# A Mamba-2 mixer inside a four-phase kernel: shorter, reordered lists for three engines in its head, and one silu tile finished during the scan

## The reference, cut to what matters

```
zxbcdt = layernorm(x) @ in_proj_w.T            # z: 512, xBC: 640, dt: 4 columns
dt  = softplus(zxbcdt[..., -4:] + dt_bias)     # one value for each token and head
xBC = silu(causal_conv1d(xBC, conv_w, 4 taps) + conv_b)
xs, B, C = split(xBC)                          # xs: 4 heads x 128
y, _ = ssd_scan(xs * dt, A * dt, B, C)         # A = -exp(A_log)
y = y + xs * D
g = y * silu(z)
g = g * rsqrt(mean(g * g) + 1e-5) * norm_w
x = x + g @ out_proj_w.T
```

## Time and profile before

| | us |
|---|---|
| median of 3 runs (lowest, highest) | 521.13 (520.99, 521.2) |
| the profiled execution | 521.09 |
| its span, first to last instruction | 519.3 |
| mean granted TensorE clock | 0.999 |

### The profile page before, as it was taken

The page is one execution under the profiler, slowest core; times in us unless marked ns, Lnnn a source line. Parts: engine busy times, 40 slices in busy tenths (PEclk is TensorE's granted clock), DMA queues, the critical chain, the costliest instruction groups (busy, mean ns, idle before and its releaser), DMA issues.

```text
span 519.3 us, 9035 instructions
## 1 busy us (share of the span) xinstructions
PE 503.5 (97%) x2950; PEld 426.7 (82%) x2951; DVE 406.6 (78%) x895; ACT 313.2 (60%) x784; POOL 145.6 (28%) x285
## 2 busy tenths in 40 slices
PE   6999999999999999999999999989999999999996
PEld 5778899999999988678888888867989768888885
DVE  5736567667666789899999899985888879899777
ACT  4656878688687754574534445899873365344342
POOL 1432434345243320020110111379554020020110
PEclk9999999999999999999999999999999999999999
DMA  7320100000000303100030000000000000000101
GB/s 278 125 81 3 40 2 2 1 1 2 2 2 8 151 2 107 42 1 1 0 141 2 2 0 1 1 2 1 1 2 1 0 1 1 1 0 1 40 2 40
DMA packets 5933, 14.17 MB, mean 27 GB/s; under 512 B 640, under 2 KB 3200, under 8 KB 5888
## 3 DMA queue, kind: packets, MB, share of 16 engines
q1 hardware_dynamic: 5888, 13.60, 7.5%
HBM read 12.55 MB, written 1.05 MB: 26 GB/s over the span
## 4 chain that ended last, share of the span: by engine, by line
PE 79%; DVE 12%; issue 3%; ACT 3%; DMA 1%; POOL 1%; SPq 0%; DVEq 0%; ACTq 0%; POOLq 0%
PE psum L172 61%; PE psum L493 4%; DVE xs L1994 2%; PE psum L525 2%; PE psum L1809 1%; PE psum L241 1%; DMA w_raw<-in_wk 1%; PE psum L1813 1%; PE psum L1819 1%; DVE f_t L1315 1%; DVE ln_stats L214 1%; DVE xn L234 1%; PE psum L1836 1%; PE psum L486 1%; ACT f_sil L1201 1%
## 5 line engine op out<-in xcount | busy, mean ns | idle before, releaser
L172 PE MATMUL psum<-xT_hl,ffn_w_hl 128*128 128x512 f32 x312 | 77.7, 395 | 0.7 <-ACT f_sil L1201 0.6
L172 PE MATMUL psum<-f_um,ffn_w_hl 128*128 128x512 f32 x288 | 72.8, 399 | 1.1 <-DVE f_t L1315 0.6
L172 PEld LDWEIGHTS psum<-xT_hl,ffn_w_hl 128*128 128x128 f32 x312 | 56.2, 188 | 13.1 <-DVE ffn_w_hl L916 1.1
L172 PEld LDWEIGHTS psum<-f_um,ffn_w_hl 128*128 128x128 f32 x288 | 53.1, 188 | 15.0 <-DVE f_um L1327 1.7
L1201 ACT ACTIVATE f_sil<-psum 128x512 f32<-128x512 f32 (+1 forms) x48 | 28.4, 596 | 49.5 <-PE psum L172 49.4
L1225 ACT ACTIVATE f_ch_hl<-f_ch 128x512 fp32r<-128x512 f32 x48 | 30.3, 631 | 41.7 <-DVE f_ch L1384 40.0
L172 PE MATMUL psum<-xT_hl,wq_hl 128*128 128x512 f32 x192 | 52.0, 407 | 0.6 <-ACT qT L593 0.6
L172 PE MATMUL psum<-wo_hl,oT_hl 128*128 128x256 f32 x384 | 50.5, 281 | 1.0 <-DVE oT_hl L726 0.6
L172 PEld LDWEIGHTS psum<-wo_hl,oT_hl 128*128 128x128 f32 x384 | 47.7, 188 | 3.5 <-DVE oT_hl L726 1.1
L593 ACT ACTIVATE qT<-psum 128x512 f32<-128x512 f32 x32 | 35.3, 1104 | 22.6 <-PE psum L172 22.4
L602 ACT ACTIVATE probs<-probs,small 120x66 f32<-120x66 f32 x120 | 39.9, 338 | 8.2 <-DVE small L703 8.2
(11 more groups left out here) (265 smaller groups left out, 1147.6 us busy)
## 6 DMA issues: line engine op xcount, KB each, us to landing
w_raw<-in_wq SPq DMA_DIRECT2D x4, 512.0 KB, 3.9
w_raw<-in_wo SPq DMA_DIRECT2D x4, 512.0 KB, 3.3
ffn_w_raw<-in_ffn SPq DMA_DIRECT2D x3, 576.0 KB, 5.8
ffn_w_raw_far<-in_ffn SPq DMA_DIRECT2D x3, 576.0 KB, 5.4
ssd_w_raw<-in_ssd SPq DMA_DIRECT2D x3, 512.0 KB, 5.3
x_resid<-in_x SPq DMA_DIRECT2D x2, 512.0 KB, 5.2
out_x<-x_resid SPq DMA_DIRECT2D x4, 256.0 KB, 2.1
w_raw<-in_wk SPq DMA_DIRECT2D x1, 512.0 KB, 6.3
```

What stands on the lines that cost most here:

```text
L172: i = e.matmul(dst, lhs(a), rhs(b), start=start and n == 0, stop=stop and n == len(TERMS) - 1, **kw)
```

## The change

Four things are edited, all in `mixer`:

- **Convolution.** DVE no longer does tap (0, 3). ACT writes bank 0 times that tap into a new tile `far` right after `last_tap(0)` (`far_taps`), and POOL adds it (`far_adds`). `silu(0)` waits for POOL's add, and bank 0 is free for `in_proj(9)` after tap (0, 2).
- **Softplus.** ACT's ln and the steps that guard it go. POOL computes it as a series in t = e / (e + 2): 15 dependent steps in place of 11, with `ident_r` and `mask_r` made ahead of them. The reciprocal follows two taps of tile 4 and waits for POOL's second step. PE puts `in_proj(16)` ahead of the cumulative sums, DVE takes them over three taps later, and ACT's order of taps and silus changes.
- **Last convolution tile.** ACT's head ends with `silu(8)`. Tile 9 gets a tanh in the scan's second chunk (`late_tanh`, i = 1), POOL turns it into a sigmoid (`late_sigmoid`, ahead of `gate(1)`) and multiplies (`late_silu`, behind it). PE's transposes of chunk 4 and ACT's second `xs_D` half, now at i = 4, wait for it.
- **POOL's order.** `join(1)` to `join(4)` move ahead of `make_xd(1)`, with `join(2)` ahead of `rhs_col`; `make_xd(3)` moves from the head into chunk 0, and 6, 7 and 8 from chunks 0, 1 and 2 (ahead of `gate`) to behind `gate` in chunk 1 (tile 6) and chunk 3 (tiles 7 and 8).

```
+            FAR = 1
+            far = at("far_taps", [P, FAR, HALF], F32, A_W)
-            DT_DONE = 11
+            DT_DONE = 15
...
-                for n in range(12, 16):
+                for n in range(12, 17):
                     in_proj(e, n)
                 e.wait_ge(S["dt_pool"], DT_DONE)
...
-                for n in range(16, 2 * NB):
+                for n in range(17, 2 * NB):
...
+                    if c == HT:
+                        e.wait_ge(S["sl"], NC)
                     for h in range(NH):
                         m = e.transpose(bank(3)[:, tile(h)], xs[:, h, tile(c)], ident)
...
+                        conv_done(e, NC - 2)
+                        keep_busy(4, 6)
+                        e.wait_ge(S["sl"], NC - 1)
+                        keep_busy(7, 6)
                         conv_done(e, NC - 1)
-                        keep_busy(4, 6)
-                        e.wait_ge(S["sl"], NC)
-                        keep_busy(7, 6)
                         e.wait_ge(S["L"], 1)
                         keep_busy(6, 6)
...
+                def far_taps():
+                    for n in range(FAR):
+                        tap = PR_CW + n
+                        e.activation(far[:, n, :], bank(IN_BANK[0]), ACT.Copy, scale=par[:, tap:tap + 1]).then_inc(S["tap"], 1)
...
                 last_tap(12)
-                e.wait_ge(S["dt_pool"], 2)
-                e.activation(L1, U1, ACT.Ln).then_inc(S["dt_act"], 1)
+                silu(2)
                 last_tap(13)
+                silu(3)
                 last_tap(14)
-                silu(2)
+                last_tap(15)
                 silu_z(16)
-                silu(3)
-                last_tap(15)
-                silu_z(17)
                 silu(4)
                 silu(5)
+                silu_z(17)
+                silu(6)
                 silu_z(18)
-                silu(6)
+                silu(7)
                 silu_z(19)
-                for i in range(7, NC):
+                for i in range(8, NC - 1):
                     silu(i)
+
+                def late_tanh():
+                    b, h = order[convs[NC - 1]]
+                    e.wait_ge(S["join"], CONVS.index(b) + 1)
+                    e.activation(xsD[:, b - 2, half(h)], xs[:, b - 2, half(h)], ACT.Tanh, scale=0.5).then_inc(S["lt"], 1)
...
+                    if i == 1:
+                        late_tanh()
-                    if i in (0, HT - 1):
+                    if i in (0, HT):
...
-                conv((0, 3), (1, 1), (1, 2))
+                conv((1, 1), (1, 2))
                 ln["lo"](e, 1)
...
-                conv((4, 1), (4, 2), (5, 1))
-                e.wait_ge(S["dt_pool"], 5)
-                e.reciprocal(R1, N1).then_inc(S["dt_dve"], 1)
-                conv((4, 3), (5, 2), (6, 1), (5, 3), (6, 2))
+                conv((4, 1), (4, 2))
+                e.wait_ge(S["dt_pool"], 2)
+                e.reciprocal(R1, TWO).then_inc(S["dt_dve"], 1)
+                conv((5, 1), (4, 3), (5, 2), (6, 1), (5, 3), (6, 2), (7, 1), (6, 3), (7, 2))
                 e.wait_ge(S["cs"], 1)
...
-                conv((7, 1), (6, 3), (7, 2), (8, 1), (7, 3), (8, 2), (9, 1), (8, 3), (9, 2), (9, 3))
+                conv((8, 1), (7, 3), (8, 2), (9, 1), (8, 3), (9, 2), (9, 3))
...
+                def far_adds():
+                    conv_read(e, 0)
+                    for n in range(FAR):
+                        d = TAPS - n
+                        out = cb_pre[:, d:HALF]
...
+                        e.tensor_tensor(out, far[:, n, 0:HALF - d], out, ALU.add).then_inc(S["gt"], 1)
...
                 select(0)
+                join(2)
                 e.wait_ge(S["rhs"], 1)
                 e.tensor_scalar(rhs_col, f32(rhs_cs), par[:, CS_FIRST:CS_FIRST + 1], None, ALU.mult).then_inc(S["rhs"], 1)
-                join(1)
+                join(3)
+                join(4)
                 make_xd(1)
-                for i in range(2, NH + 1):
-                    join(i)
                 make_xd(2)
-                make_xd(3)
+
+                def late_sigmoid():
...
+                    e.tensor_scalar(th, th, 0.5, 0.5, ALU.mult, ALU.add).then_inc(S["lt"], 1)
+
+                def late_silu():
...
+                    e.tensor_tensor(xs[:, b - 2, half(h)], xs[:, b - 2, half(h)], xsD[:, b - 2, half(h)],
+                                    ALU.mult).then_inc(S["sl"], 1)
...
-                    if c < NH - 1:
-                        make_xd(NC // 2 + 1 + c)
+                    if c == 0:
+                        make_xd(3)
+                    if c == HT - 2:
+                        late_sigmoid()
                     if c >= 1:
                         gate(c - 1)
+                    if c == HT - 2:
+                        late_silu()
+                    for i in {1: (6,), HT - 1: (7, 8)}.get(c, ()):
+                        make_xd(i)
```

More of the change, by code:

```diff
@@ L1558, in mixer @@
             carry = small[:, 32:32 + CB * (CONV - 1)].rearrange("p (b k) -> p b k", b=CB)
-            V, AV, E1, U1, L1, D1, Z1, N1, R1, SP, DT, DA, RL = (sd[:, 32 * i:32 * i + 32] for i in range(13))
+            V, AV, E1, TWO, RATIO, SQ, SERIES, R1, SP, DT, DA, RL = (sd[:, 32 * i:32 * i + 32] for i in range(12))
             AN, VE, RI = sm[:, 0:4], sm[:, 8:16], sm[:, 16:24]
@@ L1600, in mixer @@
             names = ("xda cs cm rhs mb sel gs da raw wh wl bcz ip tap ipz part join cv sl xd dt dt_dve dt_pool dt_act de L G xt X xdd wt ce Y St st1 st y g ghi glo g2 ss "
-                     "ve ri O fin bt").split()
+                     "ve ri O fin bt gt lt").split()
             S = {n: sem(f"ssd_{n}") for n in names}
@@ L1606, in mixer @@
             upto = cf[:, C_UPTO:C_UPTO + P]
-            DT_DONE = 11
+            DT_DONE = 15
+            LOG_SERIES = (2.00000001, 0.66666322, 0.40024595, 0.27965158, 0.28157778)
             NB = CB + NH
@@ L1617, in mixer, with conv_read @@
             NC = len(convs)
-            CV_ORDER = [(0, 1), (0, 2), (0, 3), (1, 1), (1, 2), (1, 3), (2, 1), (3, 1), (2, 2), (3, 2), (2, 3), (3, 3),
+            TAP_AT = [FAR + 1] + list(range(FAR + 2, FAR + 1 + NC))
+            CV_ORDER = [(0, 1), (0, 2), (1, 1), (1, 2), (1, 3), (2, 1), (3, 1), (2, 2), (3, 2), (2, 3), (3, 3),
                         (4, 1), (4, 2), (5, 1), (4, 3), (5, 2), (6, 1), (5, 3), (6, 2), (7, 1), (6, 3), (7, 2), (8, 1),
                         (7, 3), (8, 2), (9, 1), (8, 3), (9, 2), (9, 3)]
-            assert len(CV_ORDER) == TAPS * NC
+            assert len(CV_ORDER) == TAPS * NC - FAR and len(TAP_AT) == NC
             def cv_at(i, tap):
                 return CV_ORDER.index((i, tap)) + 1
+            def conv_read(e, i):
+                e.wait_ge(S["cv"], cv_at(i, TAPS if i else TAPS - FAR))
             def conv_done(e, i):
-                e.wait_ge(S["cv"], cv_at(i, TAPS))
+                if i:
+                    conv_read(e, i)
+                else:
+                    e.wait_ge(S["gt"], FAR)
             def bank_taken(e, n):
                 if n in convs:
-                    conv_done(e, convs.index(n))
+                    conv_read(e, convs.index(n))
                 else:
@@ L1892, in act @@
                 last_tap(0)
+                far_taps()
                 dt_copy(1)
@@ L1959, in act @@
                         m.then_inc(S["st1"], 1)
-                    if i in (0, HT - 1):
-                        h = i // (HT - 1)
+                    if i == 1:
+                        late_tanh()
+                    if i in (0, HT):
+                        h = i // HT
+                        if h:
+                            e.wait_ge(S["sl"], NC)
                         e.activation(xsD[:, NH - 1, half(h)], xs[:, NH - 1, half(h)], ACT.Copy,
@@ L1990, in conv @@
                         tap = par[:, PR_CW + CONV * b + CONV - 1 - d:PR_CW + CONV * b + CONV - d]
-                        e.wait_ge(S["tap"], i + 1)
+                        e.wait_ge(S["tap"], TAP_AT[i])
                         if d > 1:
@@ L2130, in carries @@
                 def carries(n, tiles, last):
-                    e.wait_ge(S["tap"], last + 1)
+                    e.wait_ge(S["tap"], TAP_AT[last])
                     b0, nb = tiles.start, tiles.stop - tiles.start
@@ L2144, in carries @@
                                     ALU.add).then_inc(S["part"], 1)
+                def far_adds():
[3 more added lines that the diff above has]
+                        out = cb_pre[:, d:HALF]
+                        if n:
+                            e.wait_ge(S["gt"], n)
+                        e.tensor_tensor(out, far[:, n, 0:HALF - d], out, ALU.add).then_inc(S["gt"], 1)
                 carries(0, slice(0, 1), 0)
+                far_adds()
                 carries(1, slice(2, CB), NC // 2 - 1)
@@ L2169, in join @@
                     e.tensor_tensor(out, out, carry[:, b, :], ALU.add).then_inc(S["join"], 1)
+                e.wait_ge(S["wl"], len(WL_ORDER))
+                e.wait_ge(S["ip"], 12)
```

(32 more changed lines are left out.)

## The result

The changed kernel takes **523.62 us** (median of 6 runs, 523.52 to 523.91) against 521.08 (6 runs, 520.97 to 521.20): 2.54 us slower, ratio 1.005, 95% interval 1.0039 to 1.006. The forecast was 523.6.

A forecast was written before the change was run, and what follows sets the result against it. The prediction took PE, nearly full in the scan, and a POOL-DVE loop that binds it from 386.38 as the bounds. gate(2) earlier, -0.6, plus the pair, +3.1, gave +2.5 on 521.1: 523.6 us, range 522.4 to 524.6.

The forecast's parts named there:

- The pair, +3.1: Scan, chunk 3: make_xd(7) and make_xd(8) directly behind gate(2) delay inverse_rms(0), and so the loop, by 3.1 us.
- the loop: Scan, POOL and DVE: gate, inverse_rms, final, split, new_state, with_skip, gate; 6.06 us long, binding PE from 386.38.
- The rival of the hidden pair: Scan: PE's distance to the loop hides the pair, leaving only PE's head gain of 0.5; 520.6 us, chance 0.07.
- the tanh's table: Scan, chunk 1: tanh needs its own table, two loads adding 1.6 to 2 us; 525.4 us, chance 0.03.
- the clock: Scan: two new PE idle times halve TensorE's clock for one chunk, some 6 us more; 529 us, chance 0.03.
- gate(2) 0.6 earlier: Scan, POOL: gate(2) comes some 0.6 us earlier, at 368.75; bounds 0 to 1.4, by how much of the head's gain arrives.
- The head, 1.4 at the exp and 0.5 at PE: End of head: first exp 1.4 us earlier, but PE's 17 fillers let only 0.5 us through to decays(1).
- Tap (0, 3), 0.4 of 0.68: Head, DVE: dropping the tap saves 0.68 us, of which 0.4 is kept because x's split waits for ACT.
- Softplus: Head: POOL's longer chain reaches a_rep at 340.5 to 341.0, PE waits 0.3 or less, cm's dependents 1.6 us later.
- Late silu and select(3): Scan: tanh, sigmoid (1.55) and multiply hidden, select(4) ending 366.0 to 366.4; select(3) in chunk 1 put at 360.6.

The follow-up runs named there:

- three tiles on ACT: Changed kernel with tiles 7 and 8 and the second `xs_D` half on ACT behind step i = 4's squares, tile 6 ahead of gate(3): 520.62 us.
- the kernel with `select(1)` first: Three tiles on ACT, without PE's last six fillers, and with POOL's select(1) ahead of make_xd(2): 519.98 us.
- the kernel before with eleven fillers: The unchanged kernel without PE's last six of 17 fillers and their wait for the first exp: 521.03 us, ratio 1.0.

## Why the prediction was right

**The pair, +3.1.** 3.10 us on POOL in the changed kernel, +3.06 on the time when moved alone, 1.57 for one of two tiles. The idle time of before lay ahead of the gate and hid nothing, and PE had no distance to the loop to give. The rival of the hidden pair is out. So are the tanh's table (no load beside it) and the clock (1.00 in 370 to 380).

**gate(2) 0.6 earlier.** It was 0.48 (368.88 against 369.36): 0.1 too much. The source is another than the sum has it. The forecast left PE 0.15 of the head's 0.5 us at `decays(3)`; 0.02 were left, and DVE's share had gone into `g_lo`. It named ACT's moved copy as a further help, but bounded the whole term by the head: 0 if the head gives nothing. The head gave next to nothing at this place and the term was still 0.48. That the size came out is in part luck. No run moved the copy back alone in the changed kernel; this is read from its trace. `final(0)` was put at 2.5 late and was 2.60; the two idle times on PE were put at 1 and 1 and were 1.09 and 0.86.

**The head, 1.4 at the exp and 0.5 at PE.** 1.29 and 0.50. The reason given, the 17 fillers, holds: in a kernel where the gain comes through (three tiles on ACT), six fewer gave 0.36 us more, and POOL's `select(1)` held another 0.28. Their start was put at 348.95 by a slip: the forecast had read 1.62 us for `decays(0)` and added 1.5. It was 349.25, 0.3 later than before. PE idled 1.19 us ahead of `decays(0)`, which went 0.1 us after `rhs_col` had ended, as forecast.

**Tap (0, 3), 0.4 of 0.68.** 0.37 on DVE and 0.39 on the time, measured in the kernel with `select(1)` first; in the changed kernel itself this gain is lost in the scan with the rest of the head's.

**Softplus.** `a_rep` started at 340.94 (forecast 340.5 to 341.0), PE waited 0.30, DVE found the sums ready. Two errors cancel in that start: POOL waited 0.84 us for the reciprocal and not up to 0.5, and its 14 steps took 0.34 us each and not 0.38. Its one price is the 1.7 us by which `cm` is later. This part was not undone by itself, so its net worth is read from the traces and not shown by a run.

**Late silu and select(3).** Tanh without a table load, hidden. The sigmoid took 0.94 us and not 1.55 (0.62 where nothing ran beside it): it was sized by `make_xd`, which takes its factor from a tile where the sigmoid has constants. The trace of before had the right row: `mask_f32r`, of the same size and with two constants, took 0.62 us, and `rhs_col`, with a factor from a tile, 1.58. No run changed the form alone. `select(4)` was put at 366.0 to 366.4 and ended at 366.97 (it took 0.88 us and not 0.44); PE took it at 367.03 without a stop. That it stayed hidden was close, and not foreseen. `select(3)` ended at 360.73, 0.13 later than put, which is what PE's gain at `decays(3)` fell short by.

**What the forecast had not seen** lay behind the pair. ACT's copy in its new place costs about 0.6 us at `g_hi(2)` once the pair is gone, and `g_lo` beside a `make_xd` 0.5; with the pair in front both were covered. For the question of what the change could have brought they were half of the answer.

## What to carry to other kernels

Where two engines hand work to each other once per iteration, time is free only on the side of the hand-over where the engine waits: 3.1 us ahead of the gate had 2.9 us of cover, the same 3.1 us behind it had none, though POOL was busy for only 28% of the kernel before. When a head is shortened, follow the gain to the engine that runs full behind it; here fillers that had been free, then a small instruction behind large ones on POOL (`select(1)`, `select(3)`), then a late copy on ACT each kept some of it. And after a large stall is taken away, read the trace again before adding up: the waits that it covered come out one by one.

## What was not expected of the hardware

In these traces, where `g_lo`, a DVE instruction with both inputs in SBUF, met nothing but a `make_xd` on POOL, only one of the two grew, and which one went with the order of their starts, a tenth of a microsecond apart. `g_lo` took 1.17 and 1.15 us in place of 0.69 when `make_xd` had begun 0.06 and 0.07 us ahead; `make_xd` took 2.01 in place of 1.56 when it began 0.11 behind (and 2.00 and 2.01 at 0.33 and 0.35 behind, where `g_lo` had met `x_dt_decay` too and took 0.89 and 0.94); with `make_xd` 0.7 us ahead neither was longer (0.69, and 3.11 for the pair). The changed kernel has a `g_lo` of 1.48, which starts 0.11 us behind POOL's two-input `x_dt_decay`. The Trainium skill ("GPSIMD Engine Reference", Key points) names the shared interface; these rows agree with it and give 0.45 to 0.8 us for one meeting. Why one of them pays and not the other, these runs do not settle.

TensorE's granted clock stayed at 1.00 through all of this: through idle times of 1.09 and 0.86 us, 1.7 us apart, and through 1.81 us ahead of `decays(1)` in the kernel before with eleven fillers. That the last six fillers are needed for the clock is not borne out here; whether the first eleven are was not tried.
